# A feed-forward in float32: two passes of seven block products instead of one pass of matmuls

## What is computed

```python
def _ff(x, W1, b1, W2, b2):
    return jax.nn.gelu(x @ W1 + b1, approximate=False) @ W2 + b2
...
mod = jax.nn.silu(c) @ W_mod + b_mod
sh_msa, sc_msa, g_msa, sh_mlp, sc_mlp, g_mlp = jnp.split(mod, 6, axis=-1)
x = x + g_msa * _attention(_modulate(_layernorm(x), sh_msa, sc_msa), W_qkv, W_out, b_out)
x = x + g_mlp * _ff(_modulate(_layernorm(x), sh_mlp, sc_mlp), W1, b1, W2, b2)
```

## Time and profile before

| | |
|---|---|
| median of three runs | 3008.34 us |
| profiled execution | 3010.88 us, span of its instructions 3009.1 us |
| granted TensorE clock | 0.996 of full speed over the span |
| busy over the span | PE 2965.8 us (99%), DVE 1986.5 (66%), ACT 1389.9 (46%), POOL 787.7 (26%) |
| DMA | 340.67 MB, mean 113 GB/s |

### The profile page before, as it was taken

How to read it: one execution, slowest core, us unless ns; L and a number is a source line. 1 busy time by engine, 2 the same in 40 slices (tenths; PEclk the granted TensorE clock), 3 DMA queues, 4 the chain that set the end, 5 groups by cost and what they waited for, 6 DMA issues and landing times.

```text
span 3009.1 us, 63179 instructions
## 1 busy us (share of the span) xinstructions
PE 2965.8 (99%) x25634; PEld 2420.6 (80%) x25634; DVE 1986.5 (66%) x2891; ACT 1389.9 (46%) x2859; POOL 787.7 (26%) x513
## 2 busy tenths in 40 slices
PE   8999999999998999999999999999999999999998
PEld 5899899999987777777777777777888888888887
DVE  4489986665535888888888888887565433343432
ACT  2266764333212777777777777776222221111111
POOL 1011110000001444444444444446553111111110
PEclk9999999999999999999999999999999999999999
DMA  5743326653596433333333333332762010010100
GB/s 179 238 152 114 110 82 243 226 202 124 179 309 182 113 96 96 86 86 86 93 91 87 93 92 97 89 86 72 252 251 99 29 30 6 29 36 29 36 15 14
DMA packets 224504, 340.67 MB, mean 113 GB/s; under 512 B 29224, under 2 KB 144072, under 8 KB 219880
## 3 DMA queue, kind: packets, MB, share of 16 engines
q1 hardware_dynamic: 215364, 330.39, 34.3%
q0 software_dynamic: 576, 6.29, 0.6%
q10 hardware_dynamic: 8292, 0.05, 0.2%
HBM read 211.15 MB, written 124.20 MB: 111 GB/s over the span
## 4 chain that ended last, share of the span: by engine, by line
PE 64%; DVE 2%; DMA 1%; ACT 0%; issue 0%; POOL 0%; SPq 0%; DVEq 0%; ACTq 0%; POOLq 0%
PE b_po L1778 16%; PE b_ps L1749 12%; PE d_pf L2252 11%; PE d_po L2263 11%; PE b_tp_act L1761 7%; PE c_po L2025 3%; PE b_tp_dve L1761 2%; DMA c_ot<-o_t 1%; DVE c_ol L2041 0%; PE d_pt L2244 0%; DVE o_first_rest L2041 0%; ACT b_p L1717 0%; DVE norm_st L1073 0%; POOL d_y L2193 0%; DVE d_gl L2320 0%
## 5 line engine op out<-in xcount | busy, mean ns | idle before, releaser
L1808 DVE TENSOR_REDUCE b_nm<-b_ps 128x1 f32<-128x1024 f32 x512 | 601.7, 1216 | 17.6 <-PE b_ps L1749 4.2
L1717 ACT ACTIVATE b_p<-b_ps,b_nm 128x1024 f32<-128x1024 f32 x512 | 564.9, 1113 | 8.6 <-DVE b_nm L1808 8.6
L1778 PE MATMUL b_po<-b_pt,b_v 128*64 128x256 f32 x4096 | 498.4, 385 | 0.8 <-DVE b_pt L1828 0.8
L1722 ACT ACTIVATE b_pt<-b_tp_act 128x512 f32<-128x512 f32 x512 | 308.2, 602 | 305.1 <-PE b_tp_dve L1761 305.1
L1828 DVE COPY b_pt<-b_tp_dve 128x512 f32<-128x512 f32 x512 | 351.1, 686 | 117.6 <-PE b_tp_dve L1761 117.5
L1761 PEld LDWEIGHTS b_tp_act<-ident,b_p 64*128 64x128 f32 x4096 | 311.7, 138 | 123.4 <-issue 100.6
L1778 PEld LDWEIGHTS b_po<-b_pt,b_v 128*64 128x64 f32 x4096 | 271.9, 136 | 128.6 <-ACT b_pt L1722 0.9
L2227 ACT ACTIVATE d_ge<-d_pf,b_t 128x512 f32<-128x512 f32 x128 | 88.2, 689 | 576.0 <-PE d_pf L2252 575.9
L1761 PE MATMUL b_tp_act<-ident,b_p 64*128 64x64 f32 x4096 | 347.7, 225 | 2.4 <-issue 2.4
L1761 PE MATMUL b_tp_dve<-ident,b_p 64*128 64x64 f32 x4096 | 348.1, 225 | 0.0
L2318 DVE CAST d_gh<-d_ge 128x512 fp32r<-128x512 f32 x128 | 65.2, 509 | 403.8 <-ACT d_ge L2227 403.6
(11 more groups left out here) (342 smaller groups left out, 6498.4 us busy)
## 6 DMA issues: line engine op xcount, KB each, us to landing
b_raw_q<-q_t SPq DMA_DIRECT2D x124, 256.0 KB, 4.2
k_t<-p_out SPq DMA_DIRECT2D x64, 256.0 KB, 2.2
q_t<-p_out SPq DMA_DIRECT2D x64, 256.0 KB, 2.3
v_n<-p_out SPq DMA_DIRECT2D x64, 256.0 KB, 3.7
b_v<-v_n SPq DMA_DIRECT2D x32, 512.0 KB, 3.9
b_raw_k<-k_t SPq DMA_DIRECT2D x124, 128.0 KB, 4.4
c_ot<-o_t SPq DMA_DIRECT2D x7, 2048.0 KB, 10.7
a_x<-x SPq DMA_DIRECT2D x32, 256.0 KB, 3.0
```

Source lines behind the costliest of these rows:

```text
L1717: act.activation(pr[k % 4][:], ps[k % 2][:], ACT.Exp, bias=nm[:, k % 4:k % 4 + 1], accum_out=rs[:, n:n + 1]).then_inc(exp_done, 1)
L1722: act.activation(dst, src, ACT.Copy).then_inc(t_out[0], 1)
L1778: mm = pe.matmul(po[rows, (blk % 2) * 2 * P:(blk % 2 + 1) * 2 * P], vt[u][:, kc, rows], pt[blk % 2][h][:, kc, :], start=(kc == 0), stop=(k ...
L1808: dve.tensor_reduce(nm[:, k % 4:k % 4 + 1], ps[k % 2][:], axis=AX.X, op=ALU.max, negate=True).then_inc(max_done, 1)
```

## The change

`mlp` is written anew. The feed-forward becomes two passes, both with `PRODUCTS`.

Pass 1 has 32 rounds v: group g of 512 rows (`g = v // 4`) times weight column set p of W1 (`p = v % 4`, 512 hidden features). A round is seven products of 12 matmuls of 256 columns; its 2 x 2 result blocks are hidden features by rows. ACT copies the first product, DVE makes five sums, ACT applies the gelu to four blocks in eight instructions of 256 columns (L2332), and POOL forms the four block sums that turn the result into the seven blocks of the next operand (L2287). SP writes the seven blocks to DRAM (`hidden_blocks`, 1.8 MB a round, two halves of SBUF in turn: `free` makes ACT and DVE wait until the stores of round v - 2 have landed). The sixth product has a PSUM bank of its own (`p_f`); in the projections it shares `p_d`. Rows of the next group are normalised, transposed and modulated beside the rounds, and their block sums, casts and rests made.

Pass 2 has 224 blocks n (8 groups x 4 sets of W2 x 7). SP loads a block (256 KB), ACT casts it, DVE makes its rest, PE multiplies it (12 matmuls of 256 columns) into one of seven PSUM accumulators. Fourteen blocks have space; DVE works seven ahead of PE (`LEAD`). After the 28th block of a group DVE drains the seven accumulators with three sums and four pairs of sum and gate product (`drained`), and POOL adds the rows. W2 is loaded into the places of W1's sets as they fall free in the last group of pass 1.

The output projection prepares the first two sets of W1 and the seven blocks of the first rows. It also makes the statistics of the second group. The other two sets of W1 are loaded at its end and prepared in rounds 0 to 2.

The core of the diff:

```diff
+                    if g == 1:
+                        load_w(sp, t, w[0], 0, w1_in, "w1")
                 else:
+                    sp.wait_ge(m_done, g * GT)
+                    sp.wait_ge(w1_in, 32)
+                    load_w(sp, t, w[1], 1, w1_in, "w1")
+                    sp.wait_ge(o_split, g * KO)
+                    sp.wait_ge(y_out[0], 16 * B)
+                    sp.wait_ge(y_out[1], 16)
+                    sp.dma_start(y1[:], y2[512:1024, :].rearrange("(a p) f -> p a f", p=P)).then_inc(y1_in, 16)
                     for n in range(GT):
+                        if n == GT - 1:
+                            sp.wait_ge(m_done, NG * GT)
+                            sp.wait_ge(w1_in, 64)
+                            load_w(sp, t, w[2], 2, w1_in, "w1")
                         sp.wait_ge(y_done, g * GT + n + 1)
                         sp.dma_start(y2[(g * GT + n) * P:(g * GT + n + 1) * P, :], yt[hf][:, n, :]).then_inc(y_out[hf], 16)
+                    sp.wait_ge(w1_in, 96)
+                    load_w(sp, t, w[3], 3, w1_in, "w1")
...
+            def beside(r):
+                if r in (11, 28):
+                    p = r // 28
+                    dve.wait_ge(w1_in, 32 * p + 32)
+                    for n in range(4):
+                        block_sum(dve, w[p], SUMS_W, n, w_sums, 4 * p)
+                if r == 18:
+                    dve.wait_ge(xm_done, GT)
+                    for n in range(4):
+                        block_sum(dve, x_first, SUMS_X, n, x_sums, 0)
+                if r in (20, 21):
+                    rest_w(0, 2 * (r - 20))
+                    rest_w(0, 2 * (r - 20) + 1)
+                if r in (25, 26):
+                    for m in (2 * (r - 25), 2 * (r - 25) + 1):
+                        dve.wait_ge(x_high, m + 1)
+                        dve.tensor_tensor(flat(rest(x_first, *GROUPS[m])), flat(raw(x_first, *GROUPS[m])), flat(high(x_first, *GROUPS[m])),
+                                          ALU.subtract).then_inc(x_rest, 1)
+                if r == 29:
...
+        PRODUCTS = ((0, 0, p_a, True), (5, 5, p_b, True), (4, 3, p_d, True), (6, 4, p_e, True),
+                    (1, 1, p_a, False), (2, 2, p_f, True), (3, 6, p_e, False))
...
+            def load_block(n):
+                v, i = block_of(n)
+                if n % 28 == 0:
+                    for u in range(2):
+                        for kind in range(2):
+                            sp.wait_ge(out_done[u][kind], 32 * 2 * (n // 28 + 1))
+                if n >= RING:
+                    sp.wait_ge(n_done, n - RING + 1)
+                if n >= 4:
+                    sp.wait_ge(r_in[n % 4], 16 * (n // 4))
...
+            for v in range(NV):
+                g, p = divmod(v, NP)
+                if p == 0 and 1 <= g < NG - 1:
+                    rstds(g + 1)
+                u = places[v % 2]
+                for n, (o, a, b, op) in enumerate(SUMS_W):
+                    if n == 0:
+                        pool.wait_ge(gelu_done, 4 * v + 3)
+                    else:
+                        pool.wait_ge(s_sums, 4 * v + n)
+                    if n == 2:
+                        pool.wait_ge(gelu_done, 4 * v + 4)
+                    pool.tensor_tensor(u[:, o, :], u[:, a, :], u[:, b, :], op).then_inc(s_sums, 1)
...
+            for v in range(NV):
+                g, p = divmod(v, NP)
+                u = places[v % 2]
+                more = g + 1 < NG
+                act.wait_ge(m_done, 7 * v + 1)
+                free(act, v, 1)
+                act.copy(u[:, 4, :], p_a[:]).then_inc(copies, 1)
+                if v:
+                    act.wait_ge(sums, 5 * v)
+                    gelu(v - 1, 1, places[(v - 1) % 2][:, 1, :])
+                if more and p == 3:
+                    high_x(g + 1, 2)
+                    high_x(g + 1, 3)
+                if v == NV - 2:
+                    for m in range(4):
+                        high_w(NP, m)
+                if more and p == 1:
+                    modulate(g + 1, 0)
+                    modulate(g + 1, 1)
+                if v == NV - 1:
+                    for n in range(LEAD):
+                        high_r(n)
+                act.wait_ge(m_done, 7 * v + 5)
...
+                free(act, v, 0)
+                gelu(v, 0, p_a)
+                act.wait_ge(sums, 5 * v + 3)
+                gelu(v, 3, u[:, 3, :])
+                if v == 0:
+                    act.wait_ge(prev.y_done, B * BT)
+                    for m in range(4):
+                        high_w(2, m)
+                if v == 1:
+                    for n in range(2):
+                        act.wait_ge(prev.y_out[n], 16 * (B - n) + 16 * GT * n)
+                    for m in range(4):
+                        high_w(3, m)
+                if more and p == 1:
+                    modulate(g + 1, 2)
+                    modulate(g + 1, 3)
+                if more and p == 2:
+                    high_x(g + 1, 0)
+                    high_x(g + 1, 1)
+                act.wait_ge(sums, 5 * v + 4)
+                gelu(v, 2, u[:, 2, :])
+            act.wait_ge(sums, 5 * NV)
+            gelu(NV - 1, 1, places[(NV - 1) % 2][:, 1, :])
+            for m in range(4):
+                high_w(NP + 1, m)
...
+            def hidden(g, p, wi, xi, out_, start):
+                for i in range(2):
+                    terms = [(a[:, 0, c, i * P:(i + 1) * P], b_[:, 0, c, :])
+                             for a, b_ in ((rest(w[p], wi), high(x[g % 2], xi)), (high(w[p], wi), rest(x[g % 2], xi)),
+                                           (high(w[p], wi), high(x[g % 2], xi))) for c in range(2)]
+                    for n, (a, b_) in enumerate(terms):
+                        mm = pe.matmul(out_[:, i * 256:(i + 1) * 256], a, b_, start=(start and i == 0 and n == 0), stop=(n == 5),
+                                       skip_group_check=True)
+                mm.then_inc(m_done, 1)
...
+            for v in range(NV):
+                g, p = divmod(v, NP)
+                if p == 0:
+                    pe.wait_ge(x_rest, 4 * g + 4)
+                if g == 0:
+                    pe.wait_ge(w_rest, 4 * p + 4)
+                for step, (wi, xi, out_, start) in enumerate(PRODUCTS):
+                    bank_free(v, step)
+                    if v == 0 and step == 5:
+                        pe.wait_ge(prev.gated_done, B * BT)
+                    hidden(g, p, wi, xi, out_, start)
+                    if g + 1 < NG and p == 1 and step in (1, 5):
+                        transposes(g + 1, step // 5 * 2)
+                        transposes(g + 1, step // 5 * 2 + 1)
+            for n in range(NB):
+                v, i = divmod(n, 7)
+                g, p = divmod(v, NP)
...
+            def beside(v, step):
+
+                g, p = divmod(v, NP)
+                at_ = (p, step)
+                if g == 0:
+                    if at_ == (0, 0):
+                        normed(1, 0)
+                        normed(1, 1)
+                    if at_ in ((0, 2), (0, 3)):
+                        if step == 2:
+                            dve.wait_ge(w1_in, 96)
+                        w_sum(2, 2 * step - 4)
+                        w_sum(2, 2 * step - 3)
+                    if at_ in ((1, 0), (1, 2)):
+                        rest_w(2, step)
+                        rest_w(2, step + 1)
+                    if at_ in ((1, 3), (1, 4)):
+                        if step == 3:
+                            dve.wait_ge(w1_in, 128)
+                        w_sum(3, 2 * step - 6)
+                        w_sum(3, 2 * step - 5)
+                    if at_ in ((2, 0), (2, 4)):
+                        rest_w(3, step // 2)
+                        rest_w(3, step // 2 + 1)
+                elif g + 1 < NG:
+                    if at_ == (0, 2):
+                        for n in range(GT):
+                            stats(g + 1, n)
+                    if at_ == (0, 3):
+                        variance(g + 1)
+                    if at_ == (0, 4):
...
+            for n in range(LEAD, NB + LEAD):
+                if n < NB:
+                    rest_r(n)
+                if n in (LEAD, LEAD + 1):
+                    for m in range(2):
+                        rest_w(NP + 1, 2 * (n - LEAD) + m)
+                if n in (LEAD + 3, LEAD + 11):
+                    w2_sums(2 + (n - LEAD) // 8)
+                if n in (LEAD + 6, LEAD + 7, LEAD + 14, LEAD + 15):
+                    k = (n - LEAD) // 8
+                    for m in range(2):
+                        rest_w(NP + 2 + k, 2 * ((n - LEAD) % 8 - 6) + m)
+                g, k = divmod(n - LEAD + 1, 28)
```

699 lines of the change are left out of this document (406 added, 293 removed).

## The result

The changed kernel takes 3001.76 us in the median of 13 runs (2999.65 to 3003.81), the kernel before 3008.34 in 13 runs beside them; the ratio is 0.9978, 95% interval 0.9971 to 0.9986. Run again in the last group of experiments it took 3002.14, ratio 0.9979 (0.9969 to 0.9989). The prediction was 3001.

What follows compares the result with a forecast made beforehand. Only the number and pace of PE's matmuls bound the feed-forward (719.1 us). Matmuls 658.6 plus waits 53 gave 711.6, 7.5 less; with +0.2 at the tail, -7.3 on the 3008.3 median: 3001 us, range 2984 to 3022.

Steps and rivals of the forecast that it cites:

- matmuls and transposes of both passes: Feed-forward if PE never waits: pass 1 336.0 us plus pass 2 322.6 us, together 658.6 against 719.1 before.
- (a): First group of pass 1: PE waits of 5.5, 4.7, 2.6 and 5.2 us from ACT's and DVE's order, 18 us.
- (b): Six later groups of pass 1: late rests, copies and transposed rows cost 1.7 us each, together 10 us.
- (c): Last round of pass 1: ACT's copy waits for stores queued behind W2 weights and first blocks, 3 us.
- (d): Start of pass 2: DVE late with sums and rests for three W2 columns, 13 us, and meeting POOL, 9; together 22.
- later groups of pass 2: Pass 2 after its start: later columns' block rests, drains and loads cost nothing.
- output projection: Stage before the feed-forward: DVE's load about unchanged, cost nothing, bounds -1.5 and +3 us.
- tail: From the last matmul to the end: 8.3 us in place of 8.1, so +0.2.
- The pace: Both passes: 256-column matmuls start 120 ns apart, so a product of 12 takes 1.44 us.
- The leads: Rival: short ACT and DVE operations overlap, so waits fall from 53 to 23 us; 2971, half way 2986; chance 0.15.
- The stores: Rival: in pass 1 ACT's copy waits for late-landing stores, 16 us more in all; slower, 3017; chance 0.20.
- The full lock: Rival: a POOL add and DVE rest exclude each other, 1.97 us a pair instead of 1.71, 15 us more; 3016; chance 0.08.

Runs made afterwards that it cites:

- the filler: The changed kernel with 16 to 24 idle PE matmuls put ahead of each of six long PE waits; 3000.90 us, ratio 0.9971 to the kernel before.

## Why the prediction was right

Point by point, in us, against the profiled executions:

| term | predicted | measured |
|---|---|---|
| matmuls and transposes of both passes | 658.6 | 652.7 |
| (a) first group of pass 1 | 18.0 | 21.7 |
| (b) groups 1 to 6 | 10 | 16 |
| (c) last round of pass 1 | 3 | 0 |
| (d) start of pass 2 | 22 | 16 |
| later groups of pass 2 | 0 | 2.8 |
| output projection | 0 | -1.9 |
| tail | +0.2 | +2.2 |

- **The pace** held: 0.24 us for two matmuls, a product 1.43. The base is 7 x 41.8 + 40.1 + 8 x 40.0 = 652.7, so the forecast was 5.9 too large: 3.3 because the 336.0 us of the projection include waits and slow matmuls of its own, 2.6 because a matmul of pass 2 takes 0.119 us and not 0.120.
- **(a)** The four waits came where they were put: 5.0, 4.0, 0.9 and 5.0 for the forecast 5.5, 4.7, 2.6 and 5.2. What is missing in the term is the half clock: most of the 6.8 us that the group lost beside its waits, of which the filler gave 4.3 back. The prediction had no such term at all. In the feed-forward before, PE never stood, but the trace before does show it in earlier stages: behind waits of 5.8 us (at 138 us) and 4.0 us (at 952 us) its clock is 0.50 too.
- **(b)** was mis-sized: 2.4 us in five groups and 4.0 in one, and not 1.7. The normalisations on DVE were costed as untouched by POOL; they took 1.46 each in place of 0.5.
- **(c)** was nothing in the changed kernel, by a margin of 0.3 us, and 2.6 to 6.0 us in kernels that moved its neighbours.
- **(d)** was too large. DVE's weight rests for block 21 ended at 2694.2, where PE would have wanted them at 2679.7: 14.5 us late and not 22. The sums of the first of the three sets had already been made in pass 1, 2.8 us that the term counts. DVE stood idle for 2.0, 2.9 and 0.7 us where 7.5 were forecast, and POOL lengthened its operations by 7 us in the durations of its timeline where 9 were forecast. The other 1.6 are half clock behind that last wait. The waits were 3.6, 1.6 and 3.0 us every seventh block and one of 2.6 for a block's rest, shorter than the 4 to 7 that the prediction named as its sign; slow stretches stood in for a part of them.
- **Later groups of pass 2** were to cost nothing. The fourth and sixth took 1.8 and 1.0 us more than the others; without the bias adds 1.9 of the 2.8 went.
- **The output projection** lost PE's waits of 1.0 and 0.6 for the transposed rows' modulation, 1.9 in all, a little past the bound of -1.5. **The tail** is two sum-and-product pairs behind each other, each product 1.25 beside POOL (rows below), where the sum counted one pair: 1.0 more. From POOL's last add to the end it is 5.3 us, where 4.3 were taken from the kernel before: another 1.0.

```profile
2989.13 1.25 DVE L2657 TENSOR_TENSOR d_gated<-d_gated,d_gate 128x512 f32<-128x512 f32 x1
...
2991.02 1.26 DVE L2657 TENSOR_TENSOR d_gated<-d_gated,d_gate 128x512 f32<-128x512 f32 x1
2991.76 2.69 SPq L2265 DMA_DIRECT2D out<-d_y_second  x4
2992.36 1.26 POOL L2301 TENSOR_TENSOR d_y_second<-d_y_second,d_gated 128x512 f32<-128x512 f32 x1 [0.62 <-DVE d_gated L2657]
```

The errors of +3.7, +6, +2.8 and +2.0 on one side and -5.9, -3, -6 and -1.9 on the other leave -2.3. The 53 us that the prediction called waits were 39.0 us of waits and 17.6 of slow matmuls and gaps too short to be listed. So the mechanism was right, that order and POOL's work make DVE and ACT late at named places; that the total came out within 1 us was luck, as each term was wrong by 2 to 6 us and one cost, the clock, was not in the sum.

**The rivals.** The leads did not cover more: the waits of (a) and (d) came at their places, and it took another order to gain 29 us. The stores did not hold the rounds: ACT's copy waited for them in 11 of 32 rounds, 23.6 us in all, and no wait of PE was for one of these copies. The full lock stays less likely than the rows' 1.71, but it is nearer than the prediction took it: in the rows of the next rows' rests (timeline of DVE and POOL, above) three rests and four sums lie between 2379.2 and 2386.9. That is 3.1 + 5.2 = 8.3 us of work in 7.7. The Trainium skill's page SBUF — State Buffer (section SBUF: two separate sides) calls the pair an exclusive lock; by it they would take 8.3, so the trace agrees but for 0.6 us. The same section counts DVE operations in a two-port mode among those that take the lock, which would cover the normalisations if they ran in one; no run here shows in which mode they were.
